# Four transformer-like stages on a 16x16 image: attention scores on 32-row tiles, normalisations in token-major form

## The reference, cut to what matters

```python
# layer 0: group norm, attention over the 256 positions, projection, residual
# layer 1: position attention (16-channel q, k), then channel attention, residuals
# layer 2: 8 heads of 16 channels over 256 positions; q and k also get an embedding of the position
scores = jnp.einsum('bhqd,bhkd->bhqk', q, k) * scale
attn = jax.nn.softmax(scores, axis=-1)
o = jnp.einsum('bhqk,bhkd->bhqd', attn, v)
o = o @ Wout + bout                      # plus the residual: x3
# layer 3: linear attention with depthwise 3x3 convolutions, then a feed-forward part
f = chan_ln(x, norm_g)
q = dwconv3x3(conv1x1(f, q_w), q_dw)     # k and v likewise
q = jax.nn.softmax(q, axis=-1) * scale   # over the 16 channels of a head
k = jax.nn.softmax(k, axis=-2)           # over the positions
ctx = jnp.einsum('bnd,bne->bde', k, v)
out = jax.nn.silu(jnp.einsum('bnd,bde->bne', q, ctx))
x = chan_ln(conv1x1(out, out_w), out_norm_g) + x
hdn = jax.nn.gelu(conv1x1(chan_ln(x, ff_g1), ff_w1), approximate=False)
return conv1x1(chan_ln(hdn, ff_g2), ff_w2) + x
```

## Time and profile before

| | |
|---|---|
| time, median of 3 runs | 92.72 us (92.59 to 92.74) |
| time of the profiled execution | 93.64 us |
| its span, first to last instruction | 91.8 us |
| PE busy | 81.8 us (89%) |
| DVE busy | 66.5 us (72%) |
| ACT busy | 53.1 us (58%) |
| POOL busy | 30.8 us (34%) |

### The profile page before, as it was taken

One profiled execution on the slowest core, in us unless ns is written; L12 is line 12 of the kernel. 1 busy time (PEld: TensorE's weight loads), 2 busy tenths in 40 slices (PEclk: granted clock), 3 DMA queues, 4 the chain that ended last, 5 costly groups with the idle time before them and its releaser, 6 DMA issues.

```text
span 91.8 us, 1634 instructions
## 1 busy us (share of the span) xinstructions
PE 81.8 (89%) x507; PEld 60.2 (66%) x510; DVE 66.5 (72%) x195; ACT 53.1 (58%) x168; POOL 30.8 (34%) x62
## 2 busy tenths in 40 slices
PE   4987997999998899899999998999999768979960
PEld 1246875576966588688676865689899535655640
DVE  1537878663685777978795998797999964887860
ACT  4002393546433118999899997992497646803830
POOL 7430598000000079400010002087876820326320
PEclk9999999995699999999999999999999999999999
DMA  1999200000000003929700000000000000000003
GB/s 28 239 323 405 115 0 0 0 7 0 0 0 4 0 0 105 286 70 255 208 0 0 0 0 0 7 0 0 0 0 4 0 0 11 0 0 4 0 3 111
DMA packets 5561, 5.01 MB, mean 55 GB/s; under 512 B 304, under 2 KB 5040, under 8 KB 5552
## 3 DMA queue, kind: packets, MB, share of 16 engines
q1 hardware_dynamic: 5408, 4.77, 16.9%
q10 hardware_dynamic: 144, 0.13, 0.4%
HBM read 3.59 MB, written 1.31 MB: 53 GB/s over the span
## 4 chain that ended last, share of the span: by engine, by line
PE 53%; DVE 20%; ACT 10%; issue 6%; POOL 6%; DMA 3%; POOLq 0%; DVEq 0%; ACTq 0%
PE bank L886 8%; PE bank L1068 6%; POOL vacc L279 4%; PE bank L1087 3%; ACT p L401 3%; PE bank L879 3%; DVE st L507 3%; DMA x<-in_x 3%; DVE nmax L700 2%; PE bank L1005 2%; PE bank L982 2%; PE bank L1148 2%; PE bank L1035 2%; PE bank L927 2%; DVE mv L511 2%
## 5 line engine op out<-in xcount | busy, mean ns | idle before, releaser
L368 ACT ACTIVATE p<-bank,nmax 128x256 f32<-128x256 f32 x32 | 14.9, 485 | 1.2 <-DVE nmax L700 1.0
L886 PE MATMUL bank<-wa,p 128*128 128x128 f32 x80 | 13.4, 290 | 0.3 <-ACT pT L375 0.3
L279 POOL TENSOR_TENSOR vacc<-vacc,p 128x240 f32<-128x240 f32 (+1 forms) x16 | 10.8, 674 | 6.8 <-ACT p L401 5.1
L700 DVE TENSOR_REDUCE nmax<-bank 128x2 f32<-128x512 f32 x16 | 10.7, 680 | 2.6 <-PE bank L1068 2.6
L886 PEld LDWEIGHTS bank<-wa,p 128*128 128x128 f32 x80 | 10.0, 149 | 2.9 <-issue 0.9
L239 POOL TENSOR_TENSOR rs<-ve,mhalf 128x2 f32<-128x2 f32 x8 | 5.6, 694 | 17.7 <-DVE ve L514 17.7
L259 POOL TENSOR_SCALAR qh<-q,wb 128x256 f32<-128x256 f32 x8 | 4.5, 587 | 17.1 <-DVE q L687 17.1
L894 PE MATMUL bank<-warm 128*128 128x512 bf16 x25 | 8.3, 446 | 1.3 <-DVE warm L520 1.2
L1148 PE MATMUL bank<-convw,fsh 128*128 128x128 f32 x72 | 9.0, 275 | 0.0
L1148 PEld LDWEIGHTS bank<-convw,fsh 128*128 128x128 f32 x72 | 8.7, 192 | 0.2
L1068 PE MATMUL bank<-k,qh 128*128 128x256 f32 x32 | 8.2, 383 | 0.4 <-ACT p L368 0.4
(11 more groups left out here) (204 smaller groups left out, 174.8 us busy)
## 6 DMA issues: line engine op xcount, KB each, us to landing
wc<-in_pack_c SPq DMA_DIRECT2D x1, 649.0 KB, 7.4
wb<-in_pack_b SPq DMA_DIRECT2D x1, 612.0 KB, 6.3
tapw<-in_taps SPq DMA_DIRECT2D x1, 576.0 KB, 8.2
stack_q<-stacks_q SPq DMA_DIRECT2D x2, 256.0 KB, 3.6
stack_k<-stacks_k SPq DMA_DIRECT2D x2, 256.0 KB, 4.0
stacks_q<-parts_q SPq DMA_DIRECT2D x2, 192.0 KB, 2.3
stacks_k<-parts_k SPq DMA_DIRECT2D x2, 192.0 KB, 2.7
wa<-in_pack_a SPq DMA_DIRECT2D x1, 320.0 KB, 3.9
```

The source lines that it names most:

```text
L279: nc.gpsimd.tensor_add(vacc[b][:, oy, ox], vacc[b][:, oy, ox], vprod[n - 1][:, iy, ix]).then_inc(s["vsum_d"], 1)
L368: nc.scalar.activation(p2[u % P2_RING][:, t, :], tiles(bank[u % S2_BANKS])[:, t, :], ACT.Exp, bias=nmax2[b][:, h, t:t + 1], accum_out=sum2 ...
L700: nc.vector.tensor_reduce(nmax2[b][:, h, :], tiles(bank[u % S2_BANKS]), AX.X, ALU.max, negate=True).then_inc(s["max2_d"], 1)
L886: last = nc.tensor.transpose(tiles(dst)[:, i, t * 128:(t + 1) * 128], src[:, t, i * 128:(i + 1) * 128], ident)
```

## The change

Layer 2 is rebuilt. Queries and keys are masked into two halves (g = 0, 1), so that each 32-row strip of the array holds one head; the four heads of a group are scored at once by products in 32-row tiles, each into its own bank (SCORE_BANKS). The maxima are written into columns of a zeroed tile, transposed by PE and added to the queries, in a row where the keys hold ones; a second product of keys and these queries gives the shifted scores already transposed, in the other four banks (SCORE_T_BANKS), and ACT exponentiates each head's bank in one instruction. v2 is padded with ones, so that the mix also gives the sums. The mix's result is evicted, transposed, divided and transposed back. The splits, the stacks in DRAM and the transposes of p are gone.

```diff
+            def group_scores(grp):
+                b, g = divmod(grp, NG)
...
+                for t in range(NT):
+                    for i in range(HG):
+                        rows = slice(QUAD * i, QUAD * (i + 1))
+                        product = nc.tensor.matmul(tiles(bank[SCORE_BANKS[i]])[:, t, :], qm2[b][rows, g, t * 128:(t + 1) * 128],
+                                                   km2[b][rows, g, :], start=True, stop=True, tile_position=(QUAD * i, 0))
...
+            def group_scores_T(grp):
...
+                pe.wait_ge(s["qa2_d"], grp + 1)
+                for t in range(NT):
+                    for i in range(HG):
+                        rows = slice(QUAD * i, QUAD * (i + 1))
+                        product = nc.tensor.matmul(tiles(bank[SCORE_T_BANKS[i]])[:, t, :], km2[b][rows, g, t * 128:(t + 1) * 128],
+                                                   qa2[b][rows, g, :], start=True, stop=True, tile_position=(QUAD * i, 0))
...
+            group_scores(0)
+            qk2(1)
+            v2_product(0)
+            v2_product(1)
+            pe.wait_ge(s["k2_d"], NG * NB)
+            max_transposes(0)
+            group_scores(1)
...
+            group_scores_T(0)
+            pe.wait_ge(s["e2_d"], 2)
+            max_transposes(1)
+            group_scores(2)
+            pe.wait_ge(s["e2_d"], HG)
+            group_scores_T(1)
+            pe.wait_ge(s["max2_d"], 2 * HG + 1)
+            group_mix(0)
+            pe.wait_ge(s["e2_d"], HG + 2)
+            max_transposes(2)
+            pe.wait_ge(s["oe2_d"], 1)
+            group_scores(3)
+            pe.wait_ge(s["e2_d"], 2 * HG)
+            group_scores_T(2)
+            pe.wait_ge(s["max2_d"], 3 * HG + 1)
+            group_mix(1)
+            pe.wait_ge(s["e2_d"], 2 * HG + 2)
+            max_transposes(3)
+            mixed_transposes(0, 0)
+            mixed_transposes(0, 1)
+            pe.wait_ge(s["e2_d"], 3 * HG)
+            group_scores_T(3)
+            o2_transposes(0)
+            group_mix(2)
+            x3_tokens(0)
+            group_mix(3)
+            mixed_transposes(1, 0)
+            mixed_transposes(1, 1)
+            f_transposes(0)
+            o2_transposes(1)
+            k_1x1(0)
+            v_1x1(0)
+            x3_tokens(1)
```

```diff
+            def y_squares(b):
+                act.wait_ge(s["yT_p"], b + 1)
+                for t in range(NT):
+                    nc.scalar.activation(ysq[b][:, t, :], tiles(LD[b], 4)[:, t, :], ACT.Square,
+                                         accum_out=yss[b][:, t:t + 1]).then_inc(s["yss_d"], 1)
```

The lists are new from there on. In the tail the stages of the two batches no longer go in pairs. POOL, ACT, DVE and PE, in that order:

```diff
+            for stage, b in ((root3, 0), (v_sums(1, 4), 0), (root3, 1), (v_sums(4, TAPS), 0), (v_sums(1, 6), 1), (root4, 0),
+                             (v_sums(6, TAPS), 1), (root5, 0), (root4, 1), (root6, 0), (root5, 1), (root6, 1)):
...
+            mixed_evac(1, 0)
+            x3T_evac(0)
+            mixed_evac(1, 1)
+            f_scale(0)
+            f_evac(0)
+            o2_evac(1)
+            for stage, b in ((shift_edges, 0), (v_products(0, 4), 0), (x3T_evac, 1), (f_scale, 1), (v_products(4, 6), 0), (f_evac, 1),
+                             (shift_edges, 1), (v_products(6, TAPS), 0), (k_exp, 0), (v_products(0, 3), 1), (q_exp, 0),
+                             (v_products(3, TAPS), 1), (ekT_evac, 0), (qT_evac, 0), (v3_evac, 0),
+                             (k_exp, 1), (o3_tanh, 0), (q_exp, 1), (gelu_table, 1), (y_squares, 0), (ekT_evac, 1), (x4_evac, 0), (qT_evac, 1), (v3_evac, 1),
+                             (o3_tanh, 1), (gelu, 0), (y_squares, 1), (hT_evac, 0), (x4_evac, 1), (gelu, 1), (y_evac, 0), (hT_evac, 1), (y_evac, 1)):
...
+            for stage, b in ((k_taps_0, 0), (x3_stats, 1), (k_taps_3, 0), (k_taps_6, 0), (k_taps_8, 0), (k_taps_0, 1), (q_max, 0), (k_sums, 0),
+                             (k_taps_3, 1), (q_norm, 0), (k_taps_6, 1), (context, 0), (k_taps_8, 1), (q_max, 1), (silu, 0), (q_norm, 1),
+                             (y_stats, 0), (k_sums, 1), (x4_sum, 0), (x4_stats, 0), (context, 1), (silu, 1), (h_stats, 0), (y_stats, 1),
+                             (y_sum, 0), (x4_sum, 1), (x4_stats, 1), (h_stats, 1), (y_sum, 1)):
...
+            for stage, b in ((conv(0, 0, TAPS), 0), (conv(1, 0, 3), 0), (f_transposes, 1), (conv(1, 3, TAPS), 0), (k_1x1, 1), (v_1x1, 1),
+                             (conv(0, 0, TAPS), 1), (ek_transposes, 0), (conv(1, 0, TAPS), 1), (q_transposes, 0), (v_transposes, 0),
+                             (ctx_product, 0), (o3_product, 0), (ek_transposes, 1), (y_products, 0), (q_transposes, 1), (x4_transposes, 0),
+                             (v_transposes, 1), (ctx_product, 1), (h_products, 0), (o3_product, 1), (h_transposes, 0), (y_products, 1),
+                             (ff_product, 0), (x4_transposes, 1), (y_transposes, 0), (h_products, 1), (keep_before_rb6, 1),
+                             (h_transposes, 1), (ff_product, 1), (y_transposes, 1)):
```

## The result

The changed kernel takes 103.56 us (102.27 to 104.0) beside 92.73 us for the kernel before: the ratio is 1.110, 95% interval 1.097 to 1.123. Slower was right, and the time lies in the range of 89.5 to 104, if only by 0.4 us. The likeliest time, 99.6 us, is 4 us too low, and 103.56 is also above the 95 to 103 that the prediction gave for its likeliest case alone. The profiled execution took 102.27 us, the fastest of its four; the other three took 103.4 to 104.0 at granted clocks of 0.932, 0.916 and 0.930.

The account below looks back on a forecast made before the run. It took the kernel for a latency chain through all engines. Terms: -0.4 to the first context, +7.3 to the second, then 0: 93.64 + 6.9 = 100.5 us profiled, less 0.9 for unprofiled runs, 99.6; range 89.5 to 104.

Parts of the forecast that it names:

- likeliest case: Whole kernel: the summed terms hold, slower at 99.6 us, 95 to 103 for this case alone; chance 0.50.
- Ahead of the attention: Embedding and first stages up to group_scores(0), forecast at 33.7: gain 0.4 us, bounds 0 to 1.3.
- Attention: Layer 2's four serial rounds of 4.13 us: x3 of batch 1 read 3.4 us sooner, batch 0 losing 0.4.
- rival of tiles that don't run at once: Row-tiled score blocks: 0.7 us more on each of five, 103.1 us; wholly serial, 111.6; chance 0.10.
- rival of a hidden round trip: Attention rounds are only their four maxima, 2.5 us, and later waits shrink: not slower, 90.2 us; chance 0.25.
- To the first context: From f(0) to batch 0's context, forecast at 72.9 against 73.31: gain 0.4 us, bounds gain 2.5 to loss 1.5.
- both waits: Ahead of the first context: f_scale(1) waits for root3(1) on POOL, and DVE waits 1.6 us for k_1x1(1).
- First to second context: Contexts of the two batches 10.0 us apart instead of 2.65, through root4(0) and three v sums: loss 7.3 us.
- whole order term: Between the contexts: the new order, holding batch 1 behind batch 0's steps, costs +7.3 us.
- Second context to the end: From the second context to y, 13.8 us as before: no difference, bounds 1.9 less to 1 more.
- The squares: Output norm's squares on ACT, behind the table load: cheap, 0.8 us for what took 0.49 + 0.25 + 0.17 on DVE.
- rival of the clock: Tail: PE's waits drop the clock to 1.2 GHz, adding 2.5 us to the sum, 102.1 us; chance 0.12.

Follow-up runs that it names:

- r1_half: a4_pairkeep with each attention maximum taken over 128 of the 256 keys: 91.34 us, ratio 0.985 to the kernel before.
- d1_before_stagger: The kernel before with only its four lists behind the convolutions put in the change's staggered order: 101.75 us at full clock, otherwise 105.4 to 106.1.
- a3_keep: The changed kernel in its own order, with some twenty warm products in PE's waits of the tail: 100.84 us, ratio 1.086 to the kernel before.
- a4_pairkeep: The changed kernel with the tail's four lists paired by batch again, plus ten warm products: 93.56 us, ratio 1.011 to the kernel before.
- a1_pool: The changed kernel with one edit in POOL's list, all v sums of batch 1 ahead of root4(0): 102.42 us, ratio 1.093 to the kernel before.
- c1_tail: The changed kernel with lists paired up to the second context, staggered from the o3 product on, with extra warm products: 99.37 us, ratio 1.074 to before.
- b2_table: a4_pairkeep with ScalarE's squares put ahead of the activation table load: 92.95 us, ratio 1.003 to the kernel before.
- f1_keep_round: e2_table_root with three warm products in the PE gap of attention's first round: 92.35 us, ratio 0.997 to the kernel before.
- e1_stats_root: a4_pairkeep with the output norm's sums on VectorE's bn_stats and batch 1's root3 earlier on POOL: 92.75 us, ratio 1.001 to the kernel before.
- e2_table_root: b2_table with batch 1's root3 earlier on POOL: 92.72 us, ratio 1.000 to the kernel before.

## Why the prediction was right, and where it was wrong

**Ahead of the attention.** group_scores(0) at 33.31, forecast 33.7. The second x2 came at 30.87, 1.0 us sooner than taken; it helps for 0.4 us only, since ACT's masked copies of k are the last to arrive (PE waits 0.75 us for them).

**Attention.** The block took 1.15 and 1.04 us against 1.07, the four maxima 2.49 against 2.48, the round 4.20 to 4.24 against 4.13: term by term as worked out. group_scores(3) at 45.92 (46.1; the start that came 0.4 us sooner makes up for rounds that are 0.1 longer), group_scores_T(3) at 50.84 (50.85), last exponential done at 54.03 (54.1), x3 of batch 0 read at 54.48 (54.35), of batch 1 at 59.84 (59.55). The rival of tiles that don't run at once is out. (The Trainium skill, "TensorE: Matmul & The Clock Gate", Part 3, has 3.07x for four row tiles; by it a block would take 3.44 / 3.07 = 1.12 us, an estimate that the prediction gives as 1.13. The trace agrees: 1.15 and 1.04.) So is the rival of a hidden round trip: DVE waits 0.61 to 0.73 us for each block, and r1_half shows that the round shortens with the maxima, by 0.65 of 1.07 us.

**To the first context.** 72.77 against 72.9: both waits that the prediction named were met, 1.66 us of ACT for root3(1) and 1.79 of DVE for k_1x1(1). Here is the first step that failed, though in the accounting. The gain of 0.4 is against a profiled execution that holds a fall of the clock, and the prediction says that part of its gain is that fall; then it takes off 0.9 us once more, as what unprofiled executions have less. The change removes the fall, so there was no 0.9 left to take off. Executions of before at full clock have a span of 90.4 to 91.1 us, most of them some 1.0 below the profiled one. None of them was profiled, but d1_before_stagger differs from before only in the order of a few entries just ahead of the contexts, and ran at a clock of 1.00 up to there: it reads x3 of batch 1 at 61.94 instead of 62.98, and its first context begins at 72.26. Against that the change is half a microsecond late at the first context, not 0.4 early.

**First to second context.** Forecast 10.0 us, measured 10.71, and at a kept clock 9.9 (a3_keep). Up to the end of POOL's three sums the chain is as forecast (8.17 us against 8.2); the 0.7 us come behind them, where the transposes and the context's product run at the low clock. The size of the whole order term, +7.3, agrees with a3_keep less a4_pairkeep, 6.8 to 7.3. Which entry decides was less certain than it reads: the prediction let root4(0) and the three v sums decide, but a1_pool shows that PE's x4_transposes(0), without those sums, holds v_transposes(1) back to all but 1.0 us of the same time, and c1_tail that the gap needs no context at all: 5.8 of the 7.3 us come up again at the silus.

**Second context to the end.** Forecast 13.8 us to y, measured 14.85 (83.48 to 98.33): just outside the bound of 14.8. The h products of batch 0, ahead of o3(1) on PE, stand in the low clock (1.91 us at 83.24, 1.13 at 92.47), so silu(1) begins 2.98 us behind the second context instead of the 1.7 of the forecast. At a kept clock it begins 1.71 us behind it, and the whole stretch takes 13.6 us (a3_keep, 83.76 to 97.33). So both stretches that came out longer did so by the clock, and the order was priced rightly.

**The clock.** A rival of its own, 0.12, at 2.5 us on top of the sum. It came: 10.2 us at a clock of 0.50 in the profiled execution, and keeping the clock took 2.7 us off the median (a3_keep), or 3.2 if the executions of a3_keep at a full clock are taken. The size was about right, and the reason given for it (PE waits for most of 20 us with one block of warm products left) fits the trace. The step that failed is the weight: its condition was met by the main case itself, since the order that parts the contexts also empties PE. It should have been a term of the sum, not a rival beside it.

**The whole.** Without the 0.9 us taken off twice the sum is 100.5 us, and at a full clock the change's order takes 100.3 to 100.4 (a3_keep). The rest, 3.2 us to the measured 103.56, is the clock: 1.8 in the profiled execution and 1.3 more in the median. Where the other three executions lost it, whether longer in the tail or in the attention too as in a3_keep, isn't shown, since they have no profile. That the stated range held is in part luck: both the likeliest case (to 103) and the rival of the clock (102.1) lie below what was measured, and only the rounding up to 104 takes it in.

**The squares.** Called cheap and put behind the table load in the sum; right for this order. What the prediction didn't say is that in a paired order with the clock kept the same place costs 0.6 us, and that a swap of two entries gives it back (b2_table).

## What to carry to other kernels

Here two batches in a chain of waits hid each other only while their steps stood in pairs in the in-order lists. Putting batch 1 behind a whole round trip of batch 0 (squares, root, sum, transposes, here some 6 us) cost that round trip once, wherever of two places the cut was made, and freeing one engine of it (POOL here, 1 to 2 of 10.8 us) brought up the next. If an edit makes TensorE wait longer, put the granted clock into the sum, and take a profile of before with a fall in it as a disturbed base: don't credit the fall twice. Before a large rewrite is given up, undo its order alone: here it was 8.4 of the 10.8 us, and the rest, with a few small edits more, came out 0.3% below the kernel before (f1_keep_round).

## What the runs showed of the hardware

The clock fell to 0.50 right behind a PE wait of 1.85 us between row-tiled blocks in two profiles, for 3.4 us in the one of b2_table. Half of the executions of e1_stats_root and e2_table_root have a mean clock of 0.975 to 0.981 and take 0.7 to 0.9 us more; with three warm bf16 products in the wait (0.82 us) all twelve kept it. The same wait stands in eight other profiles, that of the change among them, with no fall behind it: the wait alone doesn't bring the fall. In b2_table, at 0.50, the two row-tiled blocks behind the gap took 1.97 and 1.95 us instead of 1.15 and 1.04. In the tail the low clock lasted 10.2 us.

The activation table load took 1.28 us, and the next activation began at once behind it (77.83 and 79.12 in a4_pairkeep). (The Trainium skill, "ScalarE: Activation LUTs", section "What ACT_TABLE_LOAD costs", adds a drain of some 1.38 us to each switch; by it the first squares of a4_pairkeep would begin near 80.6. They began at 79.23, and the load itself began 0.02 us behind the tanh ahead of it: the trace does not show that drain.) A square between the tanh and the next load brought no load of its own (b2_table). Halving what a maximum reads, from 512 to 256 elements a row, took it from 0.62 to 0.36 us. And POOL's sums, 15 in 11.88 us in e1_stats_root, hold v_transposes(1) back in the fastest version too (0.92 us of PE's waiting in f1_keep_round); whether one of them on VectorE would give more was not tried.
